# Last expert's output kept on chip, second bias gathered one block per expert, no store of the first empty tile, and the next tile scaled in parts, in a graph and mixture-of-experts kernel

## The chip, the cores and the metric

The kernel runs on one core of one Trainium2 chip. The metric is the device time of the whole program in microseconds (us). Before the change the median of three runs is 964.02 us (962.91 to 969.46).

## The reference

A graph of 625 nodes with 768 features and 10,000 edges goes through two graph convolutions, then through one transformer layer whose feed-forward part is a mixture of eight experts with one expert per token. All is float32. Cut to the part that the change touches:

```
gate_logits = h2 @ Wg                                   # 625 x 8
w, sel = jax.lax.top_k(gate_logits, 1)
w = softmax(w)                                          # one value, so 1
hid = relu(einsum('nd,edf->enf', h2, W1) + b1[:, None, :])   # 768 -> 3072
y   = einsum('enf,efd->end', hid, W2) + b2[:, None, :]       # 3072 -> 768
moe = einsum('ne,end->nd', combine, y)
out = x + moe
```

## The kernel before, in words

The first half (graph convolutions, attention, gates) ends some 460 us into the span and is hardly touched. The second half works by **tiles**. A tile is the tokens of one expert, at most `CAP` = 128 rows; there are `E` = 8 tiles, and up to `K_OVER` = 4 more for experts with more than 128 tokens. With this data there are none: the loop over the four runs and skips its body each time (`n_over` is 0).

The 625 tokens lie in `C` = 5 blocks of `P` = 125. After the gates, DVE works out for each token its row in an HBM tensor `hs_d`; POOL scatters the tokens there (L515, five indirect DMAs), and each tile is later loaded as `hs`. Tile 0 is not loaded but chosen by a matmul with one-hot rows (`oh0`). PE turns a tile into PSUM banks 6 and 7, ACT scales it by the layer norm's weights into `hgf` (L767, six instructions), rounds it into `hgh` (L557), and DVE makes the remainder `hgl` (L825). Every fp32 product is three products of high and low parts.

A tile needs 16 **chunks** of weights, each 128 x 2304 values (1152 KB): chunks 0 to 7 of `W1` and 8 to 15 of `W2`. A chunk goes: SP starts the DMA into one of four `raw` buffers (L417, L420) as soon as DVE has finished the chunk four back; ACT rounds it into `whi` (L557, function `split_hi`); DVE subtracts into `wlo` (L825, `split_lo`); PE multiplies 18 times (L1579 for `W1`, L1593 for `W2`). In step k of a tile ACT rounds chunk k+3 and then, in its fixed order, reads the hidden block of chunk k-1 (`hid`, L792), for which PE waits with its next turns (L1566). DVE adds the first bias (`bia`, L1179) and makes `hTTl` (L823). In step 10 (`FCH + 2`) of tile t ACT and DVE do all of the next tile's scaling and splitting at once.

A tile's output stays in PSUM banks 4 and 5 until step 0 of the next tile, where ACT and DVE copy it to `ysb` (L785, L1175) and POOL stores it to `ys_d` (L530). The output of "tile -1" is stored in this way too, for a uniform loop: that is the first empty output tile, rows that tokens beyond no tile point to. After the last tile, `ysb` is copied and stored once more (L541), POOL gathers all 625 rows back into `x2` (L545, five indirect DMAs), DVE multiplies by the gate weight and adds `base` (L1214), and SP stores the result (L435).

`b2` is gathered from HBM by each token's expert: five indirect DMAs into `x2` (L520), right behind the scatter on POOL's queue; DVE adds them to `base` between tile 0 and tile 1 (L1198). The order of each engine is the order of the code; the waits are semaphores. Tiles 1 to 7 are a hardware loop (`Fori(1, E)`) on all engines, and so is the skipped loop over `K_OVER`.

## Time and profile before

| | us |
|---|---|
| median of three runs | 964.02 |
| the profiled execution | 963.17 |
| its span, from the first to the last instruction | 961.6 |
| PE busy | 867.0 (90%) |
| DVE busy | 709.2 (74%) |
| ACT busy | 545.3 (57%) |
| weight chunks for the experts (`raw<-in_L_ffn_W`) | 128 x 1152 KB, median 7.0 us from issue to landing |

The profiled execution takes 1.6 us more than its span and stands 0.85 us under the median. PE is the busiest engine; its granted clock is full in nearly all slices of the span, half of it only after pauses. In the second half of the span the 16 DMA engines are busy nearly all the time at 320 to 380 GB/s, so PE's time and the DMA's time are of about one size there, and a share of busy time doesn't say which of them sets the end. For that the waits have to be read in order of time.

### The profile page before, as it was taken

Reading aid. Unit: us, or ns where it says so; the run is one execution under the profiler, and the core shown is the slowest. Engines: PE = TensorE matmul, PEld = TensorE weight load, DVE = VectorE, ACT = ScalarE, POOL = GpSimd, SP = SyncE. Lnnn points to the kernel's source line nnn. Section 1 sums busy time; section 2 is a strip of 40 time slices with the busy share of each in tenths; the row PEclk is TensorE's granted clock in tenths of the full one; section 3 lists DMA queues with packets and bytes.
Section 4 is the critical chain, followed back from the end, with each engine's and each line's share of the span. In section 5 each row is a group of like instructions: output and inputs, shape, how many; then the busy total and the mean of one; then the engine's idle time right before and its main releaser. Section 6 shows DMA issues by size and latency. Waiting matters only on the chain.

```text
span 961.6 us, 14800 instructions
## 1 busy us (share of the span) xinstructions
PE 867.0 (90%) x5410; PEld 835.7 (87%) x5410; DVE 709.2 (74%) x1076; ACT 545.3 (57%) x753; POOL 90.9 (9%) x92
## 2 busy tenths in 40 slices
PE   7999898989997888898878899999999999999990
PEld 7999898989996667798868899999999999899990
DVE  7996265773327999744666998898979889897962
ACT  4503232352226787624447587787868788686850
POOL 2000014220003100021630000000000000000002
PEclk9999799999999998999898999999999999999995
DMA  7020008255217500230698999999999999999935
GB/s 220 10 91 1 2 1 150 69 154 101 99 50 212 197 1 1 82 99 1 219 268 322 306 354 340 371 327 381 347 350 332 342 373 331 380 337 353 350 130 177
DMA packets 117094, 197.88 MB, mean 206 GB/s; under 512 B 34599, under 2 KB 83967, under 8 KB 117046
## 3 DMA queue, kind: packets, MB, share of 16 engines
q1 hardware_dynamic: 107796, 169.08, 53.2%
q0 software_dynamic: 7424, 26.09, 8.4%
q10 hardware_dynamic: 1826, 2.06, 0.8%
q8 instruction: 32, 0.52, 0.2%
q14 instruction: 16, 0.13, 0.0%
HBM read 179.29 MB, written 17.90 MB: 205 GB/s over the span
## 4 chain that ended last, share of the span: by engine, by line
PE 51%; DVE 19%; DMA 14%; issue 7%; ACT 7%; POOL 2%; SPq 0%; DVEq 0%; ACTq 0%; POOLq 0%
PE ps L1579 13%; PE ps L1236 11%; DMA raw<-in_L_ffn_W 11%; PE ps L1593 7%; PE ps L1412 7%; DVE wlo L825 6%; PE ps L1265 4%; PE ps L1566 2%; PE ps L1472 2%; DVE pTl L825 2%; ACT whi L557 2%; ACT hgf L767 2%; DVE pr L1025 1%; DMA hs_d<-n,slot 1%; DVE pr L1032 1%
## 5 line engine op out<-in xcount | busy, mean ns | idle before, releaser
L825 DVE TENSOR_TENSOR wlo<-raw,whi 128x2304 fp32r<-128x2304 f32 x137 | 349.9, 2570 | 20.3 <-ACT whi L557 20.1
L557 ACT ACTIVATE whi<-raw 128x2304 fp32r<-128x2304 f32 x139 | 295.3, 2130 | 107.1 <-DMA raw<-in_L_ffn_W 66.1
L1579 PE MATMUL ps<-whi,hgh 128*128 128x384 f32 x384 | 135.1, 352 | 3.9 <-DVE hgl L825 2.8
L1593 PE MATMUL ps<-whi,hTTh 128*128 128x384 f32 x384 | 131.7, 343 | 0.0
L1579 PE MATMUL ps<-whi,hgl 128*128 128x384 f32 x384 | 130.8, 341 | 0.0
L1579 PE MATMUL ps<-wlo,hgh 128*128 128x384 f32 x384 | 130.0, 339 | 0.0
L1593 PE MATMUL ps<-wlo,hTTh 128*128 128x384 f32 x384 | 129.8, 338 | 0.0
L1593 PE MATMUL ps<-whi,hTTl 128*128 128x384 f32 x384 | 129.6, 338 | 0.0
L1579 PEld LDWEIGHTS ps<-whi,hgh 128*128 128x128 f32 x384 | 73.6, 192 | 4.3 <-DVE hgl L825 2.9
L1579 PEld LDWEIGHTS ps<-wlo,hgh 128*128 128x128 f32 x384 | 73.8, 192 | 0.0
L1579 PEld LDWEIGHTS ps<-whi,hgl 128*128 128x128 f32 x384 | 73.2, 191 | 0.0
L1593 PEld LDWEIGHTS ps<-wlo,hTTh 128*128 128x128 f32 x384 | 72.2, 188 | 0.0
L1593 PEld LDWEIGHTS ps<-whi,hTTh 128*128 128x128 f32 x384 | 72.1, 188 | 0.0
L1593 PEld LDWEIGHTS ps<-whi,hTTl 128*128 128x128 f32 x384 | 72.1, 188 | 0.0
L1265 PE MATMUL ps<-ohd,ohs 125*125 125x314 bf16 x400 | 58.9, 307 | 7.5 <-DVE ohd L877 5.8
L1265 PEld LDWEIGHTS ps<-ohd,ohs 125*125 125x125 bf16 x400 | 54.9, 142 | 10.3 <-DVE ohd L877 8.3
L1566 PE MATMUL ps<-ident,hid 128*128 128x128 f32 x192 | 32.6, 278 | 23.5 <-ACT hid L792 23.5
L1566 PEld LDWEIGHTS ps<-ident,hid 128*128 128x128 f32 x192 | 23.8, 142 | 30.2 <-ACT hid L792 28.6
L823 DVE SCALAR_TENSOR_TENSOR hTTl<-bia,hTTh 128x384 fp32r<-128x384 f32 x64 | 35.4, 553 | 19.4 <-ACT hTTh L557 19.4
L1179 DVE TENSOR_TENSOR bia<-ps,b1T 128x384 f32<-128x384 f32 x64 | 35.6, 556 | 15.5 <-PE ps L1566 15.5
L557 ACT ACTIVATE qh<-ps 64x125 fp32r<-64x125 f32 (+1 forms) x66 | 20.4, 309 | 44.9 <-PE ps L1412 23.0
L1449 PE MATMUL ps<-ident,pr 125*125 125x125 f32 x168 | 32.1, 307 | 10.9 <-DVE pr L1032 7.7
(264 smaller groups left out, 1744.6 us busy)
## 6 DMA issues: line engine op xcount, KB each, us to landing
raw<-in_L_ffn_W SPq DMA_DIRECT2D x128, 1152.0 KB, 7.0
hs_d<-bc POOLq DMA_DIRECT2D x13, 384.0 KB, 6.4
raw<-in_L_gnn_W SPq DMA_DIRECT2D x4, 1152.0 KB, 5.6
ys_d<-ysb POOLq DMA_DIRECT2D x9, 384.0 KB, 5.9
hs<-hs_d POOLq DMA_DIRECT2D x8, 384.0 KB, 5.5
raw<-in_L_ffn_Wv SPq DMA_DIRECT2D x6, 384.0 KB, 5.2
raw<-in_L_ffn_Wq SPq DMA_DIRECT2D x6, 384.0 KB, 5.2
raw<-in_L_ffn_Wk SPq DMA_DIRECT2D x6, 384.0 KB, 5.3
```

The source lines that it names most:

```text
L557: act.activation(out_, in_, func).then_inc(s, 1)
L767: act.activation(hgf[:, m, :], blocks(6, 128, DC, CAP)[:, m, :], ACT.Identity, scale=lnT[:, 2 * DC + m:2 * DC + m + 1], bias=lnT[:, 3 * DC ...
L823: dve.scalar_tensor_tensor(out_, in_, 0.0, hi_, ALU.max, ALU.subtract).then_inc(s, 1)
L825: dve.tensor_tensor(out_, in_, hi_, ALU.subtract).then_inc(s, 1)
L1179: dve.tensor_tensor(bia[:, k % 2, :, :], blocks(2 + k % 2, 128, JW, CAP), bcol.rearrange("p (j o) -> p j o", o=1).broadcast_to((128, JW, C ...
L1236: ins = mm(ps[0:P, bank + half, 0:HB], l, rr, start=m == 0 and i == 0, stop=m == DC - 1 and i == 2)
L1265: ins = mm(ps[0:P, m, 0:HALF], ohs[:, i % EU, m * P:(m + 1) * P], ohd[:, i % EU, :], start=i in BOUNDS, stop=i + 1 in BOUNDS)
L1412: ins = mm(ps[:, 2 * (m % 2) + half, 0:HALF], l, rr, start=c == 0 and i == 0, stop=c == DC - 1 and i == 2)
L1449: ins = nc.tensor.transpose(turned_part(u)[:, b, :], pr[:, u % PRS, b * P:(b + 1) * P], ident[0:P, 0:P])
L1566: ins = nc.tensor.transpose(blocks(2 + k % 2, 128, JW, CAP)[:, j, :], hid[0:CAP, k % 2, j * 128:(j + 1) * 128], ident[0:CAP, 0:CAP])
L1579: ins = mm(ps[0:CAP, k % 2, 0:FW], l, rr, start=m == 0 and j == 0, stop=m == DC - 1 and j == 2)
L1593: ins = mm(ps[0:CAP, 4 + half, 0:HB], l, rr, start=k == 0 and j == 0 and jj == 0, stop=k == FCH - 1 and j == JW - 1 and jj == 2)
```

## The change

There are four edits.

1. **The last expert's output stays on chip.** The tile of expert 7 becomes the last one, behind the overflow tiles, and is written out of the loop on each engine (`tile(n_over + E - 1, last=True)`); the loop over tiles is now 1 to 6, then the skipped loop over `K_OVER`, then the last tile. The routing arithmetic is changed so that slots fit this order. In the last tile nothing follows to be loaded; instead PE turns five one-hot blocks (which tokens belong to expert 7, made by five DVE instructions ahead of tile 0), ACT copies them as `ohl`. The stored rows of the earlier tiles are gathered by POOL during the last tile and added to `base` by DVE at its end. Then the output in PSUM is split into high and low parts in two halves, PE spreads it to the token blocks by the one-hot matrices (20 matmuls), DVE adds each block to `base`, and SP stores `base`.
2. **The second bias is gathered one block per expert**: one indirect DMA behind the store in each of tiles 1 to 5, and one DVE addition at the end (step 14) of each of tiles 2 to 6.
3. **The first empty output tile isn't copied and stored**; its rows, and those of one more tile, are zeroed by two more stores long before.
4. **The next tile is scaled in parts**: two of ACT's six instructions in each of steps 10, 11 and 12, `hgh` in step 12, DVE's `hgl` in step 13.

DVE's and POOL's loops over the tiles are unrolled; PE, ACT and SP keep theirs.

```diff
+BIAS_STEP = SCH - 2
+LAST_BANK = (0, 2, 6, 4, 0)
+TILE_STEPS = {FCH + 2: (0, 1), FCH + 3: (2, 3), FCH + 4: (4, 5)}
...
-            with sp.Fori(1, E) as t:
+            with sp.Fori(1, E - 1) as t:
                 weights(t, t)
...
-                    weights(e, s + E)
+                    weights(e, s + E - 1)
+            weights(E - 1, n_over + E - 1)
...
-            g.wait_ge(s_base, C)
-            for c in range(C):
-                g.indirect_dma_start(out=x2[:, c, :], out_offset=None, in_=b2[:, :],
...
-            with g.Fori(0, E) as t:
+            tile(0, first=True)
+            for t in range(1, E - 1):
                 tile(t)
+                if t <= C:
+                    if t == 1:
+                        g.wait_ge(s_base, C)
+                    c = t - 1
+                    g.indirect_dma_start(out=x2[:, c, :], out_offset=None, in_=b2[:, :],
...
-            g.wait_ge(s_yev, 2 * (n_over + E) + 2)
-            g.dma_start(ys_d[bass.ds((n_over + E) * CAP, CAP), :], ysb[0:CAP, :]).then_inc(s_ylast, 16)
+            g.wait_ge(s_yev, 2 * (n_over + E - 1))
+            g.dma_start(ys_d[bass.ds((n_over + E - 1) * CAP, CAP), :], ysb[0:CAP, :]).then_inc(s_ylast, 16)
...
+                    if last:
+                        if k == FCH + 2:
+                            a.wait_ge(s_ohT, 1)
+                            hi(ohl[:, :, :], blocks(6, 128, C, P), s_ohl)
+                        continue
+                    if k in TILE_STEPS:
+                        tile_part(t + 2, TILE_STEPS[k])
+                    if k == max(TILE_STEPS):
+                        tile_hi(DC * t + 2 * DC)
...
-            act.activation(ysb[0:CAP, 0:HB], ps[0:CAP, 4, 0:HB], ACT.Copy).then_inc(s_yev, 1)
+            tile(n_over + E - 1, last=True)
+            for half in range(2):
+                a.wait_ge(s_yhalf, half + 1)
+                hi(hg[0][:, 3 * half:3 * half + 3, :], blocks(4 + half, 128, 3, CAP), s_yh)
...
+            for c in range(C):
+                dve.tensor_scalar(oh0[:, c, :], iotac[:, :], float(CAP * (E - 1)), own[:, c:c + 1],
+                                  ALU.add, ALU.is_equal).then_inc(s_ohe, 1)
...
+            tile(E - 1, n_over + E - 1, last=True)
+            d.wait_ge(s_base2, C)
             for c in range(C):
                 d.wait_ge(s_yg[c], 16)
-                dve.scalar_tensor_tensor(x2[:, c, :], x2[:, c, :], wtok[:, c:c + 1], base[:, c, :],
+                dve.scalar_tensor_tensor(base[:, c, :], x2[:, c, :], wtok[:, c:c + 1], base[:, c, :],
+                                         ALU.mult, ALU.add).then_inc(s_yin, 1)
+            for half in range(2):
+                d.wait_ge(s_yh, half + 1)
+                part = slice(3 * half, 3 * half + 3)
+                lo(hg[1][:, part, :], blocks(4 + half, 128, 3, CAP), hg[0][:, part, :], s_yl)
...
+                bv = base[:, c, :].rearrange("p (a b) -> p a b", a=2)
+                dve.scalar_tensor_tensor(bv, wide(LAST_BANK[c], P), wtok[:, c:c + 1], bv,
                                          ALU.mult, ALU.add).then_inc(s_fin, 1)
...
-                    tile(s + E)
+                    tile(s + E - 1)
+            tile(n_over + E - 1, last=True)
+
+            pe.wait_ge(s_ohl, 1)
...
+            pe.wait_ge(s_yl, 1)
+            for c in range(C - 1):
+                spread_y(c, 0)
+            pe.wait_ge(s_yl, 2)
+            for c in range(C - 1):
+                spread_y(c, 1).then_inc(s_sel, 1)
+            pe.wait_ge(s_fin, 1)
+            spread_y(C - 1, 0)
+            spread_y(C - 1, 1).then_inc(s_sel, 1)
```

On ACT, at steps 10 to 12 of a tile, the instructions stand as follows before (`whi<-raw` are chunks 13, 14 and 15, `hgf` and `hgh` are the next tile):

```order
L557 ACTIVATE hTTh<-bia 128x384
L706 REGISTER_ALU
L557 ACTIVATE whi<-raw 128x2304
L765 REGISTER_ALU
L767 ACTIVATE hgf<-ps,lnT 128x128 x6
L770 ISA
L557 ACTIVATE hgh<-hgf 128x768
L706 REGISTER_ALU
L707 REGISTER_ALU
L557 ACTIVATE whi<-raw 128x2304
L706 REGISTER_ALU
L557 ACTIVATE whi<-raw 128x2304
```

And in the changed kernel, at the same place:

```order
L571 ACTIVATE whi<-raw 128x2304
L779 REGISTER_ALU
L781 ACTIVATE hgf<-ps,lnT 128x128 x2
L720 REGISTER_ALU
L721 REGISTER_ALU
L571 ACTIVATE whi<-raw 128x2304
L781 ACTIVATE hgf<-ps,lnT 128x128 x2
L720 REGISTER_ALU
L571 ACTIVATE whi<-raw 128x2304
L781 ACTIVATE hgf<-ps,lnT 128x128 x2
L786 ISA
L571 ACTIVATE hgh<-hgf 128x768
```

Chunks 14 and 15 have moved ahead of the last four parts and of `hgh`.

On DVE, from step 9 of tile 0 to step 1 of tile 1, before (L825 is `split_lo` and `hgl`, L1198 the second bias):

```order
L823 SCALAR_TENSOR_TENSOR hTTl<-bia,hTTh 128x384
L825 TENSOR_TENSOR wlo<-raw,whi 128x2304
L825 TENSOR_TENSOR hgl<-hgf,hgh 128x768
L825 TENSOR_TENSOR wlo<-raw,whi 128x2304 x3
L1198 SCALAR_TENSOR_TENSOR base<-x,wtok,base 125x768 x5
L1201 UNCONDITIONAL_BRANCH
L1201 ISA
L825 TENSOR_TENSOR wlo<-raw,whi 128x2304
```

And after, at the end of tile 2, the first one with a bias (L850 is `split_lo` and `hgl`, L1228 the bias, L1209 the copy to `ysb`):

```order
L848 SCALAR_TENSOR_TENSOR hTTl<-bia,hTTh 128x384
L850 TENSOR_TENSOR wlo<-raw,whi 128x2304 x4
L850 TENSOR_TENSOR hgl<-hgf,hgh 128x768
L1228 SCALAR_TENSOR_TENSOR base<-x,wtok,base 125x768
L850 TENSOR_TENSOR wlo<-raw,whi 128x2304 x2
L1209 COPY ysb<-ps 128x384
```

`hgl` stands behind chunks 13, 14 and 15 now, and one bias addition stands where five stood between tiles 0 and 1.

## Rows read from the trace of the kernel before

**Rows 1.** Windows: start:end, length, busy PE, PEld, DVE, ACT, POOL, clock, DMA share, GB/s.

```profile
491.00:560.00 69.00, 57.45 (x317) 55.72 (x318) 54.16 (x40) 43.83 (x42) 1.08 (x2) 0.95 0.94 311
560.00:895.00 335.00, 325.23 (x1903) 320.28 (x1902) 294.05 (x205) 259.96 (x239) 6.51 (x12) 0.99 1.00 351
895.00:937.00 42.00, 42.00 (x250) 41.60 (x248) 33.80 (x25) 27.62 (x30) 0.00 (x0) 1.00 0.65 226
```

**Rows 2.** Timeline of PE in tile 0: start, length, instruction, idle before and releaser.

```profile
491.09 0.55 PE L1566 MATMUL ps<-ident,hid 128*128 128x128 f32 x3 [3.39 <-ACT hid L792]
501.82 0.55 PE L1566 MATMUL ps<-ident,hid 128*128 128x128 f32 x3 [3.59 <-ACT hid L792]
510.59 0.90 PE L1566 MATMUL ps<-ident,hid 128*128 128x128 f32 x3 [3.51 <-ACT hid L792]
```

**Rows 3.** Timelines of ACT, then DVE, at the end of tile 3.

```profile
752.06 2.19 ACT L767 ACTIVATE hgf<-ps,lnT 128x128 f32<-128x128 f32 x6
...
755.16 0.96 DVE L825 TENSOR_TENSOR hgl<-hgf,hgh 128x768 fp32r<-128x768 f32 x1 [2.24 <-ACT hgh L557]
756.03 9.96 DVE L825 TENSOR_TENSOR wlo<-raw,whi 128x2304 fp32r<-128x2304 f32 x4
```

**Rows 4.** Windows, columns as in rows 1: a hole, the stretch behind it, tile 0.

```profile
759.00:761.00 2.00, 2.00 (x13) 2.00 (x12) 2.00 (x2) 0.92 (x2) 0.00 (x0) 1.00 0.31 60
761.00:775.00 14.00, 14.00 (x82) 14.00 (x81) 12.47 (x7) 9.13 (x6) 0.54 (x1) 1.00 1.07 378
486.00:504.00 18.00, 11.02 (x64) 10.34 (x63) 12.09 (x12) 9.05 (x10) 3.15 (x4) 0.98 1.04 251
```

**Rows 5.** Chain that ended last, in order of time: start, length, what.

```profile
475.55 12.49 DMA hs_d<-n,slot
...
492.20 15.75 DMA raw<-in_L_ffn_W
...
758.75 5.78 DMA raw<-in_L_ffn_W
...
769.49 8.55 DMA raw<-in_L_ffn_W
...
903.89 3.15 PE ps L1579 x18
...
907.36 3.15 PE ps L1579 x18
...
918.15 19.02 PE ps L1593 x108
...
937.19 0.57 DVE ysb L1211
...
938.43 3.98 DMA ys_d<-ysb
...
948.82 7.47 DMA x<-ys_d,slot
956.31 1.02 DVE x L1214
```

**Rows 6.** Timeline of DVE: the second bias between tiles 0 and 1.

```profile
536.02 4.73 DVE L1198 SCALAR_TENSOR_TENSOR base<-x,wtok,base 125x768 f32<-125x768 f32 x5
```

**Rows 7.** PE's sequencer after its last tile: instruction, duration ns min/median/max, first and last start.

```profile
L1602 PEldq COMPARE_BRANCH  x7: 76/208/220, 597.8 to 933.9; - x7
L1607 PEldq COMPARE_BRANCH  x4: 221/224/3625, 934.9 to 941.3; - x4
L1606 PEldq COMPARE_BRANCH  x4: 83/221/252, 938.7 to 941.7; - x4
```

**Rows 8.** Timelines of POOL and DVE at the scatter.

```profile
463.90 6.09 POOL L515 DMA_INDIRECT hs_d<-n,slot  x1 [17.25 <-DVE slot L1144]
470.30 1.20 POOL L515 DMA_INDIRECT hs_d<-n,slot  x1 [0.30 <-issue]
...
463.82 5.01 DVE L825 TENSOR_TENSOR wlo<-raw,whi 128x2304 fp32r<-128x2304 f32 x2
```

More of the change, by code:

```diff
@@ L761, in _, with tile_part @@
             split_hi(2, 0)
-            def tile_in(n_in, n_a):
+            def tile_part(n_in, part):
                 a.wait_ge(s_hgT, n_in)
-                for m in range(DC):
+                for m in part:
                     act.activation(hgf[:, m, :], blocks(6, 128, DC, CAP)[:, m, :], ACT.Identity,
@@ L769, in tile_in, with tile_hi, tile @@
                                    bias=lnT[:, 3 * DC + m:3 * DC + m + 1]).then_inc(s_hga, 1)
+            def tile_hi(n_a):
                 a.wait_ge(s_hga, n_a)
                 hi(hg[0][:, :, :], hgf[:, :, :], s_hgh)
-            tile_in(1, DC)
+            tile_part(1, range(DC))
+            tile_hi(DC)
             split_hi(3, 0)
-            def tile(t, first):
+            def tile(t, first=False, last=False):
                 for k in range(SCH):
@@ L1117, in _ @@
             kk = rt[:, 6, 16:16 + C]
+            late = rt[:, 6, 24:24 + C]
+            home = rt[:, 9, 0:C]
             tk = rt[:, 8, 0:E * K_OVER].rearrange("p (e k) -> p e k", k=K_OVER)
@@ L1142, in _ @@
             step(dve.tensor_tensor(kk, kk, far, ALU.mult))
[L1143 to L1147 removed]
+            step(dve.tensor_tensor(kk, kk, late, ALU.add))
+            step(dve.tensor_tensor(home, own, kk, ALU.add))
+            dve.tensor_copy(slot[:, :], home).then_inc(s_slot, 1)
+            dve.tensor_scalar(slot1[:, :], home, float(CAP), None, ALU.add)
             dve.tensor_copy(over[0:1, 0:1], ovend[0:1, E - 1:E])
@@ L1162, in _, with tile @@
             tile_in(1)
+            for c in range(C):
+                dve.tensor_scalar(oh0[:, c, :], iotac[:, :], float(CAP * (E - 1)), own[:, c:c + 1],
+                                  ALU.add, ALU.is_equal).then_inc(s_ohe, 1)
             split_lo(3, 0)
-            def tile(e, t, first):
+            def tile(e, t, first=False, last=False, bias=None):
                 for k in range(SCH):
@@ L1189, in tile @@
                            hTT[0][:, JW * (k - 2):JW * (k - 1), :], s_hTl2, relu=True)
-                    if k == FCH + 2:
-                        tile_in(t + 2)
-            tile(0, 0, True)
-            d.wait_ge(s_base, C)
-            for c in range(C):
-                d.wait_ge(s_b2g[c], 16)
-                dve.scalar_tensor_tensor(base[:, c, :], x2[:, c, :], wtok[:, c:c + 1], base[:, c, :],
-                                         ALU.mult, ALU.add).then_inc(s_base2, 1)
-            with d.Fori(1, E) as t:
-                tile(t, t, False)
+                    if k == BIAS_STEP and bias is not None:
+                        c = bias
+                        d.wait_ge(s_base, C)
+                        d.wait_ge(s_b2g[c], 16)
+                        dve.scalar_tensor_tensor(base[:, c, :], x2[:, c, :], wtok[:, c:c + 1], base[:, c, :],
+                                                 ALU.mult, ALU.add).then_inc(s_base2, 1)
+                    if k == max(TILE_STEPS) + 1 and not last:
+                        tile_in(t + 2)
+            tile(0, 0, first=True)
+            for t in range(1, E - 1):
+                tile(t, t, bias=t - 2 if 2 <= t < C + 2 else None)
             d.wait_ge(s_route, 1)
@@ L1555, in _, with tile @@
             keep_busy(TURN_BUSY, onesb[:, :], onesb[:, :], 3)
-            def tile(t):
-                first = isinstance(t, int)
+            def tile(t, first=False, last=False):
                 pe.wait_ge(s_hgl, t + 1)
@@ L1582, in tile @@
                         turn_hid(k - 1)
-                pe.wait_ge(s_yev, 2 * t + 2)
+                if not first:
+                    pe.wait_ge(s_yev, 2 * t)
                 for k in range(FCH):
@@ L1594, in tile @@
                                          stop=k == FCH - 1 and j == JW - 1 and jj == 2)
-                    ins.then_inc(s_used, 1)
+                        if last and k == FCH - 1:
+                            ins.then_inc(s_yhalf, 1)
+                    if not last or k < FCH - 1:
+                        ins.then_inc(s_used, 1)
                     if k == 0:
                         turn_hid(FCH - 1)
-                    if k == 1:
+                    if k == 1 and last:
+                        pe.wait_ge(s_ohe, C)
+                        for c in range(C):
+                            ins = nc.tensor.transpose(blocks(6, 128, C, P)[:, c, :], oh0[:, c, :], ident[0:P, 0:P])
+                        ins.then_inc(s_ohT, 1)
+                    elif k == 1:
                         tile_in(s_hs, 16 * t + 16, t + 1)
-            tile(0)
-            with pe.Fori(1, E) as t:
+            tile(0, first=True)
+            with pe.Fori(1, E - 1) as t:
                 tile(t)
```

68 lines of the change are left out of this document (39 added, 29 removed).

## Prediction

> **What bounds the kernel now.** I read the windows first, then PE's timeline where they show it idle, then ACT's and DVE's at the same places, the chain of work that ended last, and at the end the sequencer's own instructions at the places where the change moves them.
>
> PE is the bound of the expert part, with three kinds of leak. A chunk of `W1` takes 3.15 us, with its turns 3.47 (starts 903.89 and 907.36), and 108 matmuls of `W2` take 19.02 us, 3.17 a chunk [rows 5]. So a tile needs 8 x 3.47 + 8 x 3.17, with one more set of turns and the next tile's transposes about 54 us. The last tile runs without a gap [rows 1]. Elsewhere:
>
> - Tiles 0 and 1: in 491 to 560 PE is idle for 69 - 57.45 = 11.55 us, and the mean clock is 0.95, which is about 3.4 us of full-speed work lost at the lower of its two levels (1.2 GHz instead of 2.4) [rows 1]. 3.59 + 3.51 of the idle time are two waits of tile 0; one of 3.39 stands just before [rows 2].
> - The six boundaries into tiles 2 to 7: 335 - 325.23 = 9.77 us idle, 1.63 each [rows 1].
> - The end: PE stops at 937.17, the span ends at 961.6, so 24.4 us in which nothing multiplies. The chain there is a copy, a store (3.98), gathers issued one after another (the last lands at 956.3), an addition and the output's stores [rows 5].
>
> **Why PE waits at a boundary.** It waits for `hid`, which ACT reads behind the rounding of a chunk whose DMA is late. The cause lies some 20 us earlier. ACT's six `hgf` and `hgh` hold up `hgl` on DVE: DVE stands idle for 2.24 us and starts chunk 13 only at 756.03 [rows 3]. SP can't refill `raw` until DVE is done, so the DMA engines have a hole: 759 to 761 moved 60 GB/s where the stretch behind it moves 378 [rows 4]. That is 2 x (1 - 60/378) = 1.7 us of transfer lost. Behind the hole the engines are saturated, chunks land 8.55 us after issue instead of 5.78 [rows 5], and PE's 1.63 us of waiting is nearly the hole's size.
>
> **The change, part by part.** The sum is made against the profiled execution, 963.17 us; 0.85 us more brings it to the median of the runs.
>
> *Last output on chip, -13.4 us.* New tail from PE's last matmul (E): ACT rounds the second half, priced at the copy of the same size, 0.57 [rows 5] (the first half is ready 18/2 matmuls earlier and hides); DVE's remainder, another 0.57; the first two matmuls of the second half, 2 x 0.18 (19.02/108) and about 0.2 to start; five DVE additions of 125 x 768 at 0.95 (4.73/5 [rows 6]) to 1.02 [rows 5], 4.9; then the last store. Before, the last addition ended at 957.33 and the span at 961.6, so 4.3. Sum 0.57 + 0.57 + 0.56 + 4.9 + 4.3 = 10.9, say 11.0. Gain 24.4 - 11.0 = 13.4. PE's fifth block waits for DVE's first addition and is ready 3 us before its turn. DVE also adds the gathered rows, 5 x 0.95 = 4.8 us, before E; its last chunk was done 6 us before E, so this hides if the gathers have landed. If they haven't, all of it is added behind them. Bounds for the tail: 10 to 14.
>
> *Second bias out of tile 0, -9.9 us.* The five gathers share the queue and the engines with the first chunks: 486 to 504 moves 251 GB/s at full share [rows 4], and chunk 9 lands 15.75 us after its issue instead of 5.78 [rows 5]. Without them and the empty tile's store it should land in 7 to 8, before ACT needs it. The waits of 3.59 and 3.51 go, and with them the 3.4 of slow clock that follows long waits. The scatter, which ends at 488.04 after 12.49 us [rows 5] and holds `hTTh`, shares the engines with fewer gathers: I take 2 us off, less 0.6 for three more dependent steps in the routing, 1.4 net. 3.59 + 3.51 + 3.4 + 1.4 = 11.9, and I leave 2 for waits that stay. The five new one-hot instructions lie in a pause in which DVE waits for ACT, at no cost; without it 1.1.
>
> *Between tiles 0 and 1, -3.4.* 11.55 - 7.10 = 4.45 us idle. The five additions hold DVE for 4.73 us [rows 6], which delays four refills. They go, and so does the burst; 1 us stays.
>
> *Boundaries into tiles 2 to 5, -3.3; into 6, -1.6.* Without the hole the 1.63 goes. But each of tiles 1 to 5 now has a gather at its start, where the engines are saturated: 384 KB are 1.04 us at 378 GB/s, and up to 2.2 if the slowness of rows 4 (18 x (1 - 251/378) = 6 us lost) belongs to the five gathers, 1.2 each. PE sees this less what the freed 1.7 us leaves over. I take 0.8 us a boundary, midway between 0 and 1.63, so 4 x 0.83 = 3.3. Tile 6 has no gather: 1.6. DVE's addition (0.95) at step 14 stands in its slack, 3.17 - 2.49 (9.96/4 [rows 3]) = 0.68 a step over six steps; if that cover is gone, it costs 0.95 a tile.
>
> *Into tile 7, +5.2.* The skipped loop now stands between tiles 6 and 7. PE's sequencer leaves the tile loop at 933.9, 3.3 us ahead of the array; the first branch over the skipped body then takes 3.6 us, and the last one starts only at 941.3 [rows 7], out at 941.7. The array would run dry at 937.17 and resume at about 942: 4.8 us, plus about 1.5 at the low clock after so long a pause, plus 0.5 for the five gathers and SP's own loop, less the 1.6 of today. The late PE gives the DMA time, so I don't count the gathers' 5 x 1.04 us again.
>
> A rule of the Trainium skill speaks against this part: *Runtime: NRT & Kernel Launch*, section *Instruction fetch mechanics*: a taken branch whose target isn't in the window of fetched pages stalls until the page has come. The 3625 ns of the first branch and 221 of the others agree. By that rule a fetch amid saturated transfers would be slower than here, where none ran; by the row alone the term is +5.2, with 2.8 more (8.55 - 5.78) for a loaded queue +8.
>
> Sum: -13.4 - 9.9 - 3.4 - 3.3 - 1.6 + 5.2 = -26.4; 963.17 - 26.4 = 936.8, and about 937 us, given how little the two differ from the median.
>
> **The rivals.**
>
> *The branch costs nothing, 932 us (17%).* The 3.6 us may be the sequencer waiting for a full array queue to drain, since its end (938.5) lies just behind PE's (937.17). Then tile 7 starts like the others: 937 - 5.2. Against: the other branches took 221 ns each.
>
> *The gathers cost what they save, 945 us (20%).* Each takes 2.2 us of saturated engines, boundaries 2 to 5 stay at 1.63 (+3.3), 1 keeps another 1.5, tile 7's five gathers add 3. 937 + 7.8. For: PE and DMA are nearly level, 351 GB/s on average over 335 us against 378 at best [rows 1, 4].
>
> *POOL is locked out in the last tile, 947 us (7%).* An indirect DMA that met two of DVE's subtractions took 6.09 us and ended 1.2 after them; a free one takes 1.20 [rows 8]. In steps 2 to 9 DVE has no pause. If POOL got in only once DVE is done, at E - 6, five issues (7.5) and 7.5 to land, with the additions behind them, make the tail 21 to 22 instead of 11. Against: the bias addition between two subtractions reads only one operand from SBUF, and 30 us remain. The Trainium skill, *SBUF — State Buffer*, section *Who interferes with whom*, says just this: a DVE instruction with two SBUF inputs blocks a GpSimd one that reads SBUF, one with a single input does not. By it the gathers get in once per step, and the rival falls; the rows show only the blocking.
>
> *Slower: each jump of the skipped loop refetches (3%).* Four rounds with a jump forward and one back are eight fetches; at 3.6 + 2.8 = 6.4 us each, as above, they are 51 us instead of 3.6: 937 + 47 = 984. It decides from (36 + 3.6)/8 = 5 us per jump. Against: three of four forward branches took 221 ns [rows 7].
>
> **How the numbers follow.** The forecast itself has 50% (930 to 944: the tail's bounds, tile 0's 2 us either way, the branch up to +8). The rest is 3% for no change worth the name (waits that only move elsewhere, 955 to 970). Runs of this kernel tell about 1% from no change, 9.6 us. Faster by more: 50 + 17 + 20 + 7, less 1 for their edges, 93%; within 1%: 4%; slower 3%. The range leaves out the last two, half of the lock-out rival and the far ends of the first three: 928 to 948.
>
> **What would show it.** Right: PE's first wait in tile 0 near 2 us and none over 1.5 behind it; no DVE wait for `hgh` over 1 us and no DMA hole at a tile's end; a single pause of PE of 4 to 5 us between tiles 6 and 7 with the branch beside it; 11 us between the last weight matmul and the end. Wrong: PE waits for `hid` over 1.5 us at boundaries 1 to 5 (gathers), no pause before tile 7 (branch), DVE waiting for a gather at the end (lock-out), or chunks 8 and 9 still landing after 10 us or more (then tile 0's waits had another cause).

## The result, and the profile after

The changed kernel takes 974.12 us (median of 14 runs, 967.89 to 980.9) where the kernel before takes 964.18 (14 runs on the same chip, 960.86 to 969.46). The ratio is 1.0098, with a 95% interval of 1.0074 to 1.0122: **about 1% slower**, where 937 us and 3% faster had been predicted. The profiled execution takes 974.38 us, its span is 972.9 against 961.6.

The span of each stretch shows where the time went. A tile ends here where DVE copies its output (`ysb`); tiles 0, 6 and 7, where DVE comes late or not at all, end with PE's last matmul:

| stretch | before | after | difference | predicted |
|---|---|---|---|---|
| up to PE's first chunk of tile 0 | 474.2 | 476.2 | +2.0 | 0 |
| tile 0 | 68.0 | 58.2 | -9.8 | -9.9 |
| tile 1 | 58.9 | 58.0 | -0.9 | -3.4 |
| tiles 2 to 5 | 223.8 | 241.3 | +17.5 | -3.3 |
| tile 6 | 56.0 | 53.6 | -2.4 | -1.6 |
| tile 7, with the way into it | 56.3 | 73.3 | +17.0 | +5.2 |
| behind the last weight matmul | 24.4 | 12.3 | -12.1 | -13.4 |
| sum | 961.6 | 972.9 | +11.3 | -26.4 |

Tiles 0 and 6 and the end came out nearly as worked out; tiles 2 to 5 and 7 carry 32.6 of the 37.7 us between forecast and span. First the windows of the changed kernel, one for each of tiles 1, 2, 6 and 7 (start:end, length, busy PE, PEld, DVE, ACT, POOL, granted clock of PE, DMA share, GB/s; PEld is PE's loading of weights):

```profile
534.00:592.00 58.00, 54.42 (x321) 53.30 (x320) 49.12 (x34) 43.76 (x40) 3.53 (x3) 1.00 1.01 346
592.00:652.00 60.00, 56.55 (x319) 55.67 (x319) 50.22 (x35) 43.61 (x40) 3.55 (x3) 0.94 0.98 332
...
833.00:889.00 56.00, 54.34 (x322) 53.66 (x320) 49.42 (x35) 43.99 (x41) 0.56 (x1) 1.00 0.99 342
889.00:961.00 72.00, 59.81 (x321) 58.66 (x322) 49.11 (x38) 35.40 (x32) 10.46 (x6) 0.91 0.75 229
```

Tiles 1 and 2 have a gather of `b2` at their start, and PE is idle for 3.5 us in each; in tile 2 the mean granted clock falls to 0.94 as well. Tile 6 has no gather and runs at the full clock; the 1.7 us of idle time in its window are the start of the wait for the skipped loop. Tile 7 has five gathers of `ys_d`: 12 us idle in its window, and a clock of 0.91.

PE's timeline: its waits over 0.6 us behind the front in tile 0, at the start of tile 2, and in tile 7 (start, length, instruction, idle before it and releaser), answers to [rows 2]:

```profile
492.24 0.90 PE L1609 MATMUL ps<-ident,hid 128*128 128x128 f32 x3 [2.57 <-ACT hid L809]
...
609.21 0.90 PE L1609 MATMUL ps<-ident,hid 128*128 128x128 f32 x3 [3.34 <-ACT hid L809]
...
894.12 0.68 PE L1622 MATMUL ps<-whi,hgh 128*128 128x384 f32 x1 [6.79 <-issue]
...
914.86 0.67 PE L1609 MATMUL ps<-ident,hid 128*128 128x128 f32 x3 [2.04 <-ACT hid L809]
923.09 0.55 PE L1609 MATMUL ps<-ident,hid 128*128 128x128 f32 x3 [2.98 <-ACT hid L809]
928.82 0.90 PE L1609 MATMUL ps<-ident,hid 128*128 128x128 f32 x3 [2.05 <-ACT hid L809]
```

Tile 0 keeps one wait, of 2.57 us where "near 2" was predicted. All waits of PE for `hid` behind the front sum to 28.9 us in 11; less 2.57 in tile 0 and 7.07 in tile 7, 19.3 us lie in tiles 1 to 5, the ones with a gather, 3.9 each. The long wait of each is between 3.17 and 4.24 us.

How one of these boundaries goes is in the chain of work that ended last (start, length, what), to be read against the 5.78, 8.55 and 3.15 of [rows 5]:

```profile
592.37 0.56 DVE ysb L1209
592.92 2.48 DVE wlo L850
...
595.59 11.05 DMA raw<-in_L_ffn_W
...
608.69 0.48 ACT hid L809
609.17 0.04 issue
609.21 0.90 PE ps L1609 x3
610.12 5.32 PE ps L1622 x18
```

A weight chunk takes 11.05 us to land. The same entry at the other four boundaries reads 11.36, 11.92, 11.68 and 11.38. Behind the wait 18 matmuls take 5.32 us instead of 3.15, the clock having fallen to its lower level in between (1.2 instead of 2.4 GHz). The five boundaries differ in this: behind the waits of tiles 1 to 5 the 18 matmuls take 3.15, 5.32, 5.50, 4.16 and 5.14 us, so 7.5 us are lost to the clock in all, and none in tile 1. The five gathers, and then two windows, at a boundary without a gather (tile 6) and behind a gather (tile 2):

```profile
L548 POOL DMA_INDIRECT x<-in_L_ffn_b,eidx x5: 2411/2428/2438, 536.2 to 775.1; - x5
...
DMA to landing us min/median/max: 12.0/12.6/13.1
```

```profile
833.00:848.00 15.00, 15.00 (x91) 14.85 (x90) 12.99 (x11) 12.00 (x11) 0.56 (x1) 1.00 1.06 382
600.00:606.00 6.00, 5.76 (x33) 5.12 (x32) 5.42 (x4) 2.54 (x3) 0.00 (x0) 1.00 1.07 261
```

For 6 us behind the gather the DMA engines move 261 GB/s instead of 382. The hole of [rows 4] (60 GB/s), which edit 4 was to close, is closed: `hgl` follows the chunk before it at once (765.34, no idle time before it) instead of after 2.24 us [rows 3].

At the skipped loop, PE's sequencer (duration in ns min/median/max, first and last start), then the window behind it and one further on in tile 7:

```profile
L1659 PEldq COMPARE_BRANCH  x4: 221/224/5344, 885.2 to 893.3; - x4
```

```profile
894.00:898.00 4.00, 3.88 (x12) 3.89 (x13) 0.89 (x1) 0.00 (x0) 0.00 (x0) 0.50 1.04 387
904.00:922.00 18.00, 14.07 (x74) 13.37 (x73) 12.24 (x10) 8.69 (x10) 6.05 (x2) 0.91 1.01 251
```

The first branch takes 5.34 us (3.63 in [rows 7]), the other three 0.22 each. PE is idle for 6.79 us and then runs at half clock for four more. The second window holds the gathers of `ys_d`: 251 GB/s once more. The end of the chain (12.3 us from the last weight matmul to the span's end, against 24.4 before):

```profile
941.61 19.01 PE ps L1637 x108
960.62 1.80 PE ps L1667 x10
...
962.51 2.87 DVE base L1257 x3
...
966.31 0.93 DVE base L1257
```

### The profile page after: what moved, and what is told of

Same layout as the page of the kernel before. It is cut to its first block, busy times and chain, and to the rows that moved or that the text cites. A ratio compares the mean times of both kernels' runs of the same rounds, so it can differ in the third digit from the quotient of the medians.

```text
span 972.9 us, 14520 instructions
## 1 busy us (share of the span) xinstructions
PE 884.9 (91%) x5429; PEld 853.5 (88%) x5429; DVE 712.8 (73%) x1088; ACT 543.6 (56%) x747; POOL 99.3 (10%) x91
## 3 DMA queue, kind: packets, MB, share of 16 engines
q0 software_dynamic: 7344, 25.70, 8.2%
## 4 chain that ended last, share of the span: by engine, by line
PE 66%; DVE 15%; DMA 9%; issue 5%; ACT 5%; DVEq 1%; SPq 0%; ACTq 0%
PE ps L1637 20%; PE ps L1622 14%; PE ps L1279 12%; DMA raw<-in_L_ffn_W 7%; PE ps L1455 6%; DVE wlo L850 3%; PE ps L1515 2%; PE ps L1609 2%; DVE pTl L850 2%; PE ps L1308 1%; DVE pr L1050 1%; PE ps L1492 1%; DMA xs<-in_x 1%; DVE pr L1057 1%; DVE ohs L901 1%
## 5 line engine op out<-in xcount | busy, mean ns | idle before, releaser
L850 DVE TENSOR_TENSOR wlo<-raw,whi 128x2304 fp32r<-128x2304 f32 x137 | 350.2, 2569 | 22.6 <-ACT whi L571 19.3
L1622 PE MATMUL ps<-whi,hgh 128*128 128x384 f32 x384 | 139.7, 364 | 9.6 <-issue 6.8
L1622 PE MATMUL ps<-wlo,hgh 128*128 128x384 f32 x384 | 134.1, 349 | 0.0
L1622 PE MATMUL ps<-whi,hgl 128*128 128x384 f32 x384 | 134.0, 349 | 0.0
L1622 PEld LDWEIGHTS ps<-whi,hgh 128*128 128x128 f32 x384 | 77.2, 201 | 10.0 <-issue 7.1
L1622 PEld LDWEIGHTS ps<-wlo,hgh 128*128 128x128 f32 x384 | 77.0, 201 | 0.0
L1622 PEld LDWEIGHTS ps<-whi,hgl 128*128 128x128 f32 x384 | 76.4, 199 | 0.0
L1609 PE MATMUL ps<-ident,hid 128*128 128x128 f32 x192 | 34.4, 291 | 29.1 <-ACT hid L809 28.9
```

The lines of the kernel that those rows point to most:

```text
L850: dve.tensor_tensor(out_, in_, hi_, ALU.subtract).then_inc(s, 1)
L1609: ins = nc.tensor.transpose(blocks(2 + k % 2, 128, JW, CAP)[:, j, :], hid[0:CAP, k % 2, j * 128:(j + 1) * 128], ident[0:CAP, 0:CAP])
L1622: ins = mm(ps[0:CAP, k % 2, 0:FW], l, rr, start=m == 0 and j == 0, stop=m == DC - 1 and j == 2)
```

## The experiments

The question was why a gather that moves 375 KB (the prediction's 384 KB is the size of 128 rows), 1 us of the engines' time at full rate, makes chunks land 3 us late and costs a tile 5 to 6 us. Two smaller ones stood beside it: what the skipped loop costs, and whether the terms that came out right are right for the reason given. Ratios are to the kernel before, run on the same chip, with their 95% intervals.

### Where the price lies: no gathers, early ones, plain transfers, fewer rows

**n_none** leaves out the five gathers of `b2` (the second bias is missing in the output):

```diff
-                    g.indirect_dma_start(out=x2[:, c, :], out_offset=None, in_=b2[:, :],
-                                         in_offset=bass.IndirectOffsetOnAxis(ap=eidx[:, c:c + 1], axis=0)
-                                         ).then_inc(s_b2g[c], 16)
```

> The changed kernel without its five gathers of the second bias; the additions stay (they add an old block, so the second bias is missing from the output). Theory G: the gathers at the start of tiles 1 to 5 cause the waits of about 4 us and the slow clock of about 1 to 2 us behind each, so these go and the median falls from 974 to 950 (946 to 955), with PE idle under 0.5 us at the boundaries into tiles 1 to 5, as at the one into tile 6. Rival D: DVE's addition at step 14 and the unrolled loops cause them; then it stays at 970 or more.

945.38 us, ratio 0.978 [0.972, 0.983]. PE's waits for `hid` from 535 to 870 shrink to 0.8 us in all. So the five gathers cost 974.1 - 945.4 = 28.7 us, 5.7 each. The two kernels ran on different occasions; by their ratios it is 31 us, 6.2 each. The prediction had 0.8 each, and 2.2 as the upper bound.

**n_early** puts the five gathers back behind the scatter, where they stood before the change:

```diff
+            g.wait_ge(s_base, C)
+            for c in range(C):
+                g.indirect_dma_start(out=x2[:, c, :], out_offset=None, in_=b2[:, :],
```

> The changed kernel with the five gathers moved back behind the scatter, where they stood before; the additions stay one per tile. Theory G: boundaries into tiles 1 to 5 run without waits, tile 0 gets back its two waits of 3.5 us and the slow clock, in all some 8 to 10 us: 959 (955 to 963). Rival D: 970 or more.

953.98 us, ratio 0.987 [0.982, 0.992], 20 us less than with the gathers spread out. Tile 0's waits are back (5.50, 0.83 and 4.72 us), and there are none at the boundaries. Five gathers in one heap cost 8.6 us over none, spread out 28.7: edit 2, in this form, makes things worse.

**n_direct** replaces each gather by a plain DMA of 125 rows of another HBM tensor, on the same queue at the same place (the bias is not the right one), and **n_112** gathers only the first 112 of a block's 125 rows (the other 13 tokens get no second bias):

```diff
-                    g.indirect_dma_start(out=x2[:, c, :], out_offset=None, in_=b2[:, :],
+                    g.dma_start(x2[:, c, :], x1_d[c * P:(c + 1) * P, :]).then_inc(s_b2g[c], 16)
```

```diff
-                    g.indirect_dma_start(out=x2[:, c, :], out_offset=None, in_=b2[:, :],
-                                         in_offset=bass.IndirectOffsetOnAxis(ap=eidx[:, c:c + 1], axis=0)
+                    g.indirect_dma_start(out=x2[0:112, c, :], out_offset=None, in_=b2[:, :],
+                                         in_offset=bass.IndirectOffsetOnAxis(ap=eidx[0:112, c:c + 1], axis=0)
```

> The changed kernel with each gather of the second bias replaced by a plain DMA of the same 125 rows of 3 KB from one HBM tensor, at the same place (the values are not the bias). If the bytes cost what they cost (1.04 us each at 378 GB/s), the waits shrink from 4 to 2 us and the median is 958 to 965. If the address list of an indirect DMA is what slows the engines, it is 950 to 955. If 125 rows in any form do it, it stays at 974.

> The changed kernel with each gather of the second bias cut to the first 112 rows of its block (13 tokens of each block get an old row instead). Theory S: 125 rows are dealt to the 16 DMA engines unevenly and 112 = 16 x 7 evenly, so the waits fall from 4 to under 2 us and the median to 955 to 962. Otherwise 10% fewer rows take 10% off the gathers' price: 971 to 974.

n_direct: 950.73 us, 0.987 [0.980, 0.994]; the transfers land after 7.5 us instead of 12.6. n_112: 951.61 us, 0.985 [0.979, 0.991], landing after 8.2. Taking away a tenth of the rows takes away nearly four fifths of the price: n_112 stands 6.2 us above n_none of the same occasion, 1.2 a gather. So neither the bytes nor POOL's work on an indirect DMA are what is dear.

### What about 125 rows is dear

**n_128** is complete: each gather of `b2` takes 128 rows, three more than needed, through three zeroed indices. The same done to the gathers of `ys_d` too is **n_all128**:

```diff
-        eidx = sb("eidx", [P, C], I32)
+        eidx = sb("eidx", [128, C], I32)
...
-                    [("x2", [P, C, D], F32), ("base", [P, C, D], F32)])
+                    [("x2", [128, C, D], F32), ("base", [P, C, D], F32)])
...
-                    g.indirect_dma_start(out=x2[:, c, :], out_offset=None, in_=b2[:, :],
+                    g.indirect_dma_start(out=x2w[:, c, :], out_offset=None, in_=b2[:, :],
...
+            step(dve.memset(eidx[:, :], 0))
```

> The changed kernel, complete, with the gathers of the second bias widened from 125 to 128 rows (three more entries in the list of rows, all 0, into three partitions that nobody reads). More bytes than in the changed kernel. Theory S (125 rows are dealt unevenly, 128 and 112 evenly): as fast as with 112 rows, 948 to 955 where the changed kernel takes 974. If it was the 10% of bytes, or the cut itself: 974 to 976.

> As the run before, and the five gathers of the stored outputs in the last tile have 128 rows too. Theory S: they slow the last tile in the same way (two waits of 3.0 and 2.1 us and the low clock behind them), so another 4 to 8 us go: 942 to 949. If the last tile's waits come from the loop ahead of it alone, no change against the run before.

n_128: 948.11 us, 0.984 [0.980, 0.989]. It moves more bytes than the changed kernel and is 26 us faster (24.5 by the ratios). n_all128: 938.31 us, 0.974 [0.970, 0.977], 10 us more from the last tile alone. In n_128 the gathers' landing and the chain at the same boundary (592 us) read:

```profile
DMA to landing us min/median/max: 7.8/8.2/8.2
```

```profile
592.58 8.16 DMA raw<-in_L_ffn_W
...
602.81 0.48 ACT hid L810
603.29 0.05 issue
603.34 0.55 PE ps L1612 x3
603.88 3.15 PE ps L1625 x18
```

The chunk lands after 8.16 us instead of 11.05, and the 18 matmuls behind it run at full clock, 3.15 us.

**n_distinct** gathers 125 rows that are all different (of `hs_d`, by `slot`; the bias is not the right one), to see whether it matters that all tokens read the same eight rows of `b2`:

```diff
-                    g.indirect_dma_start(out=x2[:, c, :], out_offset=None, in_=b2[:, :],
-                                         in_offset=bass.IndirectOffsetOnAxis(ap=eidx[:, c:c + 1], axis=0)
+                    g.indirect_dma_start(out=x2[:, c, :], out_offset=None, in_=hs_d[:, :],
+                                         in_offset=bass.IndirectOffsetOnAxis(ap=slot[:, c:c + 1], axis=0)
```

> The changed kernel with its five gathers of 125 rows at the same places, but the rows come from hs_d by each token's slot (625 different rows) instead of from b2 by each token's expert (8 rows that all tokens share); the bias is therefore not the right one. It tells apart what about a gather is dear. Theory (125 rows, however they lie, are dealt unevenly over the DMA engines): as the changed kernel, 974, within 970 to 978, landing 12 to 13 us. Rival (the rows are dear since 125 descriptors read the same 8 rows of HBM): 948 to 952, as with the plain transfer, landing 7 to 8 us; then the gain by 112 or 128 rows would be unexplained.

973.23 us, 1.006 [1.003, 1.009], landing after 12.2: it does not matter.

**n_120, n_115 and n_113** gather 120, 115 and 113 rows of each block, with the edit of n_112 and another number:

> The changed kernel with only the first 120 rows of each block of b2 gathered; the last five tokens of a block get no second bias. 120 is no multiple of 16, but 15 divides it. Theory of divisors (a gather goes to as many engines, at most 16, as divide its rows; 125 rows go as 25 rows on each of 5 engines, and 120 would go as 8 rows on each of 15): as with 112 rows, 951.6, so 948 to 956, landing 8 us. Theory of multiples of 16 (any row count that isn't one is dear): as with 125 rows, 970 to 976, landing 12 us. The Trainium skill, DMA: Bandwidth & Descriptors, section Why a DMA increments its semaphore by 16 and not by 1, states the rule of the divisor; by it this run is cheap.

> The changed kernel with only the first 115 rows of each block of b2 gathered; the last ten tokens of a block get no second bias. Theory of divisors: 5 engines with 23 rows each, nearly as with 125 rows (5 engines with 25): 968 to 974, landing 11 to 12 us, though fewer bytes move than with 120 rows. If the bytes or the count of rows in themselves decided: 950 to 953, between 112 and 120 rows.

> The changed kernel with only the first 113 rows of each block of b2 gathered; the last twelve tokens of a block get no second bias. 113 is prime. Theory of divisors: all 113 rows, 347 KB, go to one engine; at the 378 GB/s over 16 engines of a saturated stretch, 23.6 each, that is 14.7 us of that one engine, against 3.3 for 25 rows and 0.9 for 7. A boundary between tiles then costs some 11 us more than with 125 rows and the five together 40 to 60: 1010 to 1035 us. Theory of multiples of 16 or any other in which 113 is as uneven as 125: 970 to 974. One row more than in the run with 112 rows (951.6) would thus cost nothing or over 50 us.

| rows | largest divisor up to 16 | rows on each | us | ratio | landing, us | packets of POOL's queue |
|---|---|---|---|---|---|---|
| 112 | 16 | 7 | 951.61 | 0.985 [0.979, 0.991] | 8.2 | 6624 |
| 120 | 15 | 8 | 954.02 | 0.986 [0.980, 0.992] | 8.7 | 6624 |
| 128 | 16 | 8 | 948.11 | 0.984 [0.980, 0.989] | 8.2 | 6624 |
| 115 | 5 | 23 | 970.87 | 1.004 [1.001, 1.006] | 11.8 | 7264 |
| 125 | 5 | 25 | 974.12 | 1.010 [1.007, 1.012] | 12.6 | 7344 |
| 113 | 1 | 113 | 1021.44 | 1.058 [1.053, 1.064] | 28.2 | 10864 |

"Largest divisor" is the number of engines if the rows are dealt evenly, so 125 rows go to five engines. The three runs with 7 or 8 rows on each can't be told apart by their intervals; above them the times rise with the rows on each engine, and not with the bytes: one row more than 112 costs 70 us. The packets (those of the queue that POOL's DMAs go through) say the same without any time. Against the 6224 of n_none they are 80 a gather with 112, 120 and 128 rows and for the plain DMA, 208 with 115, 224 with 125 and 928 with 113: 8 more for each further row on one engine from 23 to 25 and to 113. No view shows the engines singly, but in n_113 a window comes near to it. PE's wait in the tile with the first gather, the chunk that held it up, and two windows:

```profile
562.47 0.90 PE L1609 MATMUL ps<-ident,hid 128*128 128x128 f32 x3 [14.03 <-ACT hid L809]
```

```profile
536.38 23.45 DMA raw<-in_L_ffn_W
```

```profile
555.00:560.00 5.00, 0.00 (x0) 0.00 (x0) 0.00 (x0) 0.09 (x1) 0.00 (x0) 0.50 0.07 27
553.00:555.00 2.00, 0.00 (x0) 0.00 (x0) 0.00 (x0) 0.00 (x0) 0.00 (x0) 0.50 0.61 205
```

For 5 us next to nothing works but the DMA engines at a share of 0.07, near one sixteenth, and they move 27 GB/s; a sixteenth of the 378 of a full stretch [rows 4] is 23.6. This is what it looks like when one engine is finishing its part of the weight chunks, behind 113 rows of the gather (347,136 bytes, an estimated 14.7 us at that rate), and until it has, no chunk is complete. With 125 rows it would be five engines with 25 rows each: 76,800 bytes, 3.3 us, against 0.9 to 1.0 for 7 or 8 rows. The difference of 2.3 is what the chunks should land later by; it was 11.05 - 8.16 = 2.9. The Trainium skill says the same: *DMA: Bandwidth & Descriptors*, section *Why a DMA increments its semaphore by 16 and not by 1*, has a DMA run on the largest number of engines up to 16 that divides the outermost dimension of both sides, and notes that some plain copies from GpSimd are dealt evenly nonetheless. All six counts and n_direct agree with it. What the rows don't explain is that the mean DMA share stays at 1.07 while 261 GB/s are moved. Perhaps a packet's recorded time holds waiting too; that isn't shown, but the share alone would have hidden the loss here.

### The skipped loop

**n_noloop** leaves the loop over `K_OVER` out on every engine (with this data it never ran a tile). **n_skip** keeps it, but behind one branch:

```diff
-            with pe.Fori(0, K_OVER) as s:
-                with pe.If(s < n_over):
-                    tile(s + E - 1)
+            with pe.If(n_over > 0):
+                with pe.Fori(0, K_OVER) as s:
+                    with pe.If(s < n_over):
+                        tile(s + E - 1)
```

> The changed kernel without the loop over the four overflow tiles on any engine (none is used with these inputs; the count is still loaded). Theory L: the loop costs PE the pause of 6.8 us between tiles 6 and 7 and some 2 us at the low clock: 974 falls to 964 to 967. Rival: the gathers in the last tile make PE wait by what the pause had given them, and it stays within 4 us: 970 to 974.

> The changed kernel, complete, with one edit: on each engine the loop of four skipped tiles stands inside one branch, so it is not run. The gathers keep their 125 rows. Theory (the loop's four branches and reads of registers on PE and DVE are what costs 6 to 7 us at the boundary into the last tile): as with the loop taken out altogether, 967 to 969. Rival (code of the last tile has to be fetched when a branch jumps over the loop, at one far branch's price of 3.6 us on PE): 971 to 972.

n_noloop: 967.55 us, 1.005 [1.002, 1.008]; n_skip: 970.29 us, 1.003 [1.000, 1.006]. By the ratios the loop costs 5 to 6 us. The two can't be told apart by their intervals, though their traces differ: in n_noloop PE does not stand idle at that place at all, and meets longer waits for `hid` behind it (5.58 and 4.35 us, beside the gathers of `ys_d`), in n_skip it stands idle for 4.4 us, beside a branch of 6.33 us on its sequencer. One branch over the whole loop is not free, which is seen again below.

### Do the terms that came out right hold

**b_parts** is the kernel before with edit 4 alone (the next tile scaled in parts). **b_128** is the kernel before with all ten gathers of 128 rows. **b_both** has both:

```diff
+TILE_STEPS = {FCH + 2: (0, 1), FCH + 3: (2, 3), FCH + 4: (4, 5)}
...
-                    if k == FCH + 2:
-                        tile_in(t + 2, DC * t + 2 * DC)
+                    if k in TILE_STEPS:
+                        tile_part(t + 2, TILE_STEPS[k])
+                    if k == max(TILE_STEPS):
+                        tile_hi(DC * t + 2 * DC)
```

> The kernel before with the fourth edit alone: the next tile is scaled in parts in steps 10 to 12 and its low part made in step 13. Theory H (the burst makes a hole in the transfers and PE's 1.63 us of waiting at each boundary): the six waits go, 8 to 10 us faster than before, ratio 0.990 to 0.992. Rival: the engines are saturated anyway, ratio 0.997 to 1.001.

> The kernel before, complete, with one edit: all ten gathers take 128 rows in place of 125. There the five gathers of b2 stand together behind the scatter, in tile 0, and the five of ys stand alone behind the last tile. Theory (a gather of 125 rows holds up the weight chunks that are under way with it): tile 0's three waits of PE (10.5 us together) shrink to 2 or 3 us together, and the ys gathers, which land alone, gain a few us on their own landing: 964 less 8 less 3 is 953, between 948 and 958. Rival (the price arises only where a gather meets saturated weight loads at a tile's boundary, and tile 0's waits are due to the weights' rounding order): 960 to 964. Rival (in the changed kernel the gain of 128 rows came from another thing than the deal over the engines, such as the placing of the buffers): no change, 964.

> The kernel before, complete, with two edits: the next tile scaled in parts (edit 4 of the change) and all ten gathers of 128 rows. The output of the last expert still goes over HBM, the five gathers of b2 stand in tile 0. Theory (the forecast's terms for the tail and for tile 0 are right, less what the wide gathers give there too): the two edits alone gave 12 and 7 us, so 946, and 944 to 950, some 8 to 12 us behind the fastest version. Rival (the tail and tile 0 bring nothing, since other waits take their place): 938, level with the fastest version.

b_parts: 951.68 us, 0.987 [0.984, 0.991]. In windows against [rows 1] and [rows 4]:

```profile
560.00:895.00 335.00, 334.50 (x1979) 331.85 (x1978) 307.15 (x214) 271.61 (x252) 6.51 (x12) 1.00 1.03 364
759.00:761.00 2.00, 2.00 (x13) 2.00 (x12) 1.51 (x2) 1.05 (x2) 0.00 (x0) 1.00 1.07 374
```

The hole of 60 GB/s is gone, and with it all but 0.5 of the 9.77 us of PE's idle time at the six boundaries. The reading of [rows 3] and [rows 4] was right, and what it is worth is 12 us, more than the 9.8: PE's waits on the way into tile 1, which edit 4 touches too, also fall, from 4.35 us to 2.43.

b_128: 958.01 us, 0.993 [0.990, 0.996], 7 us. Of tile 0's three waits (10.5 us) one of 4.90 stays, and the end behind PE's last matmul is 23.0 us instead of 24.4, the gathers of `ys_d` landing after 4.6 us instead of 7.6. b_both: 942.69 us, 0.978 [0.974, 0.982], where the two alone add up to about 946.

**best1** and **best2** are one kernel run on two occasions, complete: the changed kernel with ten gathers of 128 rows and the branch of n_skip.

> The changed kernel, complete, with two edits: all ten gathers (five of b2, five of ys) take 128 rows in place of 125 (the three extra rows are read by zeroed indices and not used), and on each engine the loop of four skipped tiles stands inside one branch, so that it is not run at all when there are no overflow tiles. Theory (the deal of the gathers over the DMA engines costs about 36 us, the skipped loop about 6.5 us, and these two add up): the widened gathers alone gave 938.3, the loop taken out gave 6.6 us over the changed kernel, so 932 us, between 929 and 935, a ratio to the kernel before of about 0.967. Rival (the branch that takes the loop's place costs the queues of the engines as much as the loop did, a refetch of code that lies far ahead): 938, no gain over the widened gathers alone. The trace should have the idle time of PE at the boundary into the last tile at 1 to 3 us instead of 6.8, and the first two chunks of that tile at the full clock.

> The fastest version again (the changed kernel with 128-row gathers and the skipped loop inside one branch), to compare it with b_both on one chip: 938, within 934 to 941, a ratio to the kernel before near 0.970.

best1: 938.28 us, 0.970 [0.966, 0.973]. best2, beside b_both: 934.61 us, 0.969 [0.966, 0.972]. This is the fastest version. It is 8 us, 0.9%, ahead of b_both, so edits 1 to 3 and the branch together bring that much once the gathers are cheap. The five scatters into `hs_d` still have 125 rows in every version; widening them was not tried. The branch did less than expected (932): over n_all128 the gain is 0.4%, and the intervals overlap. The profile of best2 shows why (PE's sequencer, then PE):

```profile
L1665 PEldq COMPARE_BRANCH  x1: 6672/6672/6672, 862.0 to 862.0; - x1
```

```profile
869.02 0.68 PE L1629 MATMUL ps<-whi,hgh 128*128 128x384 f32 x1 [4.66 <-issue]
```

The single branch takes 6.67 us, longer than the first one in the loop (5.34), so PE still stands idle for 4.66 us. *Runtime: NRT & Kernel Launch*, section *Instruction fetch mechanics*, in the Trainium skill has a taken branch stall when its target isn't in the fetched pages, until a DMA has fetched the page. The dear branches agree with it (3.63 us where the DMA engines moved 53 GB/s on average, in 934 to 942 before the change [rows 7]; 5.34, 6.33 and 6.67 amid weight loads at over 300), though no run here changes the distance or the load alone.

## Why the prediction was wrong

- **The second bias out of tile 0, predicted -9.9: right, in part by luck.** Tile 0 became 9.8 us shorter. Both waits of [rows 2] that I had counted are gone, and n_early, with the gathers back in tile 0, has long waits there again, so the cause is right. But the idle time fell by 7.9 us (10.49 to 2.57), and 1.9 are left for everything else, where I had counted 7.1 less 2 for waits that stay, and 3.4 + 1.4 for the clock and the scatter.
- **Between tiles 0 and 1, -3.4: it was -0.9.** The waits of 1.13, 1.80 and 1.42 us are gone, but the first gather's wait of 3.17 stands in their place. In n_none PE waits 0.43 us there, so the cause was right and the gather ate the gain.
- **The last output on chip, -13.4: right in kind, 1.3 too much.** It was -12.1: the way from PE's last weight matmul to the end is 12.3 us, not 11.0. From 960.62 to DVE's first addition it is 1.89 us (1.70 counted), and the five additions run without a gap in 4.72 (4.9 counted). What I had wrong is the last stretch, from the last addition to the end: 5.7 us, where I took over the 4.3 of before. SP issues ten stores for the five blocks, and needs longer for them than DVE for the additions. Before, DVE waited for a gather between additions, and SP's last issue ended 0.8 us after the last of them (958.13 against 957.33); now it ends 2.2 us after (969.48 against 967.23). Timelines of DVE and SP after the change, then of SP before it:

```profile
962.51 4.72 DVE L1257 SCALAR_TENSOR_TENSOR base<-ps,wtok,base 125x768 f32<-125x768 f32 x5 [0.78 <-PE ps L1667]
963.56 5.92 SPq L444 DMA_DIRECT2D out_x<-base  x10
...
950.63 7.50 SPq L435 DMA_DIRECT2D out_x<-x  x10
```

- **The hole at a tile's end, -1.6 a boundary: right,** and a little small: tile 6, which has no gather, became 2.4 us shorter, and b_parts gave 12 us for all the boundaries.
- **The gathers at the boundaries, +0.8 each: this is the step that failed.** I took a gather as 384 KB of the mean bandwidth, 1.04 us, with 2.2 as the upper bound. n_none measured 5.7 each (28.7 us in all). The price of these transfers wasn't in their bytes, but in what they put on their most loaded engine: a weight chunk landed after 11.05 us beside 25 rows on each of five engines, 8.16 beside 8 rows on each of sixteen, and 23.45 beside 113 rows on one. With 112 rows the gather did cost about what the bytes say, 1.2 us each. The upper bound was built from the same mean rate, by dividing the 6 us lost in [rows 4] among five gathers, and so had no room for that. Of the 5.7 about 3.9 are PE's waits and 1.5 the lower clock behind them (7.5 us over the five boundaries, none of it at the first).
- **The way into tile 7, +5.2: too small by 2.** Idle time 6.79 instead of 4.8, since the branch took 5.34 us and not 3.63, and the low clock 2.0 (36 matmuls in 8.32 us instead of 6.3) instead of 1.5; less the 1.6 of before that is 7.2. The value for a loaded queue that stood beside it, +8, was a little nearer.
- **The five gathers in tile 7, counted as hidden at 0.5: also wrong, and by the same cause.** Waits of 2.04, 2.98 (on a chunk that took 14.66 us to land) and 2.05 us, 1.2 of slow clock behind the last (a chunk of 4.35) and 1.6 in 904 to 922 (18 us at 0.91) are 9.9 us; with the 7.2 that is the 17.0 of the table. I had argued that PE's late start gives the DMA time. n_all128 gets 10 us back over n_128, and what it changes is these five gathers.
- **The front, +2.0,** was not foreseen. PE's first chunk of tile 0 starts at 476.2 in this profile, and between 474.7 and 479.1 in those of n_all128 and best1, whose front differs from it by two small instructions; so single executions scatter by more than this, and it stays open.

Of the rivals, *the gathers cost what they save* named the right place, and the waits for `hid` at boundaries 1 to 5 were on the list of signs of being wrong; but its size (945, with 2.2 a gather) came from the mean bandwidth too, and not from the deal of the rows. *The branch costs nothing* fell: the branch went on until 890.5, 3.2 us after PE's last matmul of tile 6, and PE stood idle for 6.79. *POOL is locked out* fell: two of its gathers took 3.09 and 3.15 us instead of 1.25, but all were issued by 910.4, 42 us before DVE's additions at 952.62. *Each jump refetches* fell: one of four branches was dear. The slower side had 3% on a mechanism that didn't occur, and none on the one that did. Had the range taken in the landing time of the gathers in [rows 5] seriously (a scatter of 125 rows in 12.49 us, against 5.78 for a chunk three times its size), it would have reached higher, though that row had five scatters in a heap and would not have told the deal from the heap.

## What to carry to other kernels

Price a transfer placed among saturated ones by its load on the busiest of the DMA engines: look at the row count before the bytes. A gather of 125 rows cost 5.7 us here. One of 128 rows cost 0.5 by the medians ((948.1 - 945.4)/5) and 1.3 by the ratios, and the intervals allow anything from nothing to 2.6; one of 112 rows cost 1.2. So padding an index list to a multiple of 16 is the first thing to try. The dearest count tried was the prime 113. Small transfers of this uneven kind that are spread out over many saturated places can cost more than the same ones in a heap at one place (28.7 us against 8.6), since each place pays for a wait and mostly for the clock behind it. Whether that holds for 128 rows too was not tested.

## What the runs showed of the hardware

- An indirect DMA of R rows of 3 KB behaves as if dealt to the largest divisor of R up to 16: landing after 8.2 us (112, 128), 8.7 (120), 11.8 (115), 12.6 (125) and 28.2 (113), amid weight loads. The deal itself is inferred from these, the times, the packet counts and the window of n_113.
- POOL's issue of such a gather at a tile's start is longer too, with more rows on an engine: a median of 2.18 us for 128 rows, 2.43 for 125, 3.59 for 113.
- A plain DMA of 125 rows from POOL's queue at the same place has none of this: 7.5 us to landing.
- The first branch over the skipped loop's body on PE's sequencer took 3.63 us with nearly idle DMA engines and 5.34 with busy ones, the next ones 0.22; one branch over the whole loop took 6.33 and 6.67 us.
- Behind a wait of 3 to 4 us PE's clock fell to its lower level at four of five boundaries and stayed up at one (3.17 us).
